# The last attention group of a cross-attention and mixture-of-experts kernel written out step by step, its row plan and output products moved, and one bf16 cast given to ScalarE

## What is computed

```python
qp = einsum('bld,ed->ble', layernorm(x), Wq)
idx = argmax(einsum('bld,bmd->blm', qp, ctx), axis=-1)      # one context row for each x row
mkv = take(ctx, idx) @ Wkv.T                                # one key and one value head, 16 wide
attn = softmax(qh @ mk.T / 4)                               # 16 heads, queries against all rows
x = x + (attn @ mv) @ Wc.T
# mixture of experts: 8 experts, 2 for each row
h = layernorm(x)
topk_w, sel = top_k(softmax(h @ router_w.T), 2)
y = (h @ w1[e, 512:].T) * silu(h @ w1[e, :512].T)           # 256 -> 512
x = x + sum over the two e of topk_w * (y @ w2[e].T)        # 512 -> 256
```

## Time and profile before

| | |
|---|---|
| median of 3 runs | 381.35 us (380.42 to 387.86) |
| the profiled execution | 383.68 us |
| its span, first to last instruction | 381.9 us |
| mean granted TensorE clock | 0.968 |
| TensorE busy | 335.8 us (88%) |
| VectorE, ScalarE, GpSimd busy | 206.0, 186.9, 191.8 us |

### The profile page before, as it was taken

One profiled execution on the slowest core, in us unless ns is written; L12 is line 12 of the kernel. 1 busy time (PEld: TensorE's weight loads), 2 busy tenths in 40 slices (PEclk: granted clock), 3 DMA queues, 4 the chain that ended last, 5 costly groups with the idle time before them and its releaser, 6 DMA issues.

```text
span 381.9 us, 7576 instructions
## 1 busy us (share of the span) xinstructions
PE 335.8 (88%) x2303; PEld 231.9 (61%) x2304; DVE 206.0 (54%) x686; ACT 186.9 (49%) x344; POOL 191.8 (50%) x212
## 2 busy tenths in 40 slices
PE   2999979989988888699899799999999999999950
PEld 2975644445544433477666577777777777777740
DVE  4668664546887757477786244434444344444420
ACT  2544347795885963354633244444444444444420
POOL 3300248777675772625873545554555554545430
PEclk9999999999989969899999899999999999999996
DMA  8999712234253365905223323333333232333321
GB/s 246 393 406 409 272 44 70 80 100 155 98 180 113 113 213 132 346 2 146 52 41 89 66 36 55 58 56 56 56 55 52 44 52 48 56 56 56 43 27 14
DMA packets 35626, 43.77 MB, mean 115 GB/s; under 512 B 3248, under 2 KB 28208, under 8 KB 35600
## 3 DMA queue, kind: packets, MB, share of 16 engines
q1 hardware_dynamic: 27024, 32.58, 24.6%
q0 software_dynamic: 7488, 10.39, 16.8%
q10 hardware_dynamic: 1088, 0.46, 0.5%
HBM read 27.49 MB, written 15.93 MB: 114 GB/s over the span
## 4 chain that ended last, share of the span: by engine, by line
PE 65%; DVE 9%; issue 8%; POOL 6%; DMA 6%; ACT 3%; ACTq 0%; POOLq 0%; DVEq 0%
PE ps L1528 25%; PE ps L1539 12%; POOL low L475 5%; PE ps L1546 5%; PE ps L1382 4%; PE ps L1252 3%; PE ps L1342 2%; DMA X<-rows,idx 2%; PE ps L1241 2%; PE ps L1514 2%; DMA pT<-in_Wq 2%; PE ps L1283 1%; PE ps L1323 1%; DVE oh L924 1%; PE ps L1350 1%
## 5 line engine op out<-in xcount | busy, mean ns | idle before, releaser
L522 POOL DMA_INDIRECT out_x<-xn,idx x39 | 62.3, 1596 | 88.6 <-ACT xn L676 84.1
L475 POOL TENSOR_TENSOR low<-raw,W 128x256 bf16<-128x256 f32 x96 | 67.2, 730 | 50.3 <-ACT W L575 47.2
L1528 PE MATMUL ps<-W,kb 128*128 x312 | 83.5, 410 | 0.1
L682 ACT ACTIVATE uT<-ps 128x512 f32<-128x512 f32 x39 | 23.3, 597 | 84.7 <-PE ps L1528 84.7
L1528 PEld LDWEIGHTS ps<-W,kb 128*128 128x128 f32 x312 | 57.1, 190 | 12.4 <-issue 0.5
L1122 DVE TENSOR_TENSOR uT<-uT,ps 128x512 f32<-128x512 f32 x39 | 26.8, 686 | 56.9 <-ACT uT L682 56.9
L1126 DVE TENSOR_TENSOR kb<-ps,mT 128x512 fp32r<-128x512 f32 x39 | 27.0, 692 | 46.8 <-ACT mT L688 46.8
L498 POOL DMA_INDIRECT X<-rows,idx x39 | 39.0, 1000 | 24.0 <-issue 11.3
L1528 PE MATMUL ps<-W1lo,kT 128*128 x156 | 40.4, 382 | 0.0
L814 DVE TENSOR_REDUCE mx<-ps 128x8 f32<-128x616 f32 x32 | 25.3, 795 | 17.9 <-PE ps L1283 17.8
L596 ACT ACTIVATE pT<-ps 77x2048 f32<-77x2048 f32 x16 | 30.0, 1873 | 7.5 <-PE ps L1323 7.5
(11 more groups left out here) (200 smaller groups left out, 537.1 us busy)
## 6 DMA issues: line engine op xcount, KB each, us to landing
raw<-in_w SPq DMA_DIRECT2D x8, 1536.0 KB, 16.4
lows<-low SPq DMA_DIRECT2D x48, 128.0 KB, 1.7
W1lo<-lows SPq DMA_DIRECT2D x8, 512.0 KB, 4.4
rows<-xr SPq DMA_DIRECT2D x4, 528.0 KB, 3.5
X<-in_x SPq DMA_DIRECT2D x4, 512.0 KB, 7.4
out_x<-X SPq DMA_DIRECT2D x4, 512.0 KB, 4.4
pT<-lows SPq DMA_DIRECT2D x8, 256.0 KB, 5.9
X<-rows,idx POOLq DMA_INDIRECT x39, 2.8
```

Of the source, the lines that this page charges most:

```text
L475: op = pool.tensor_tensor(low[:, n % LR, part], raw[:, n + 2, part], W[:, n, part].bitcast(F32), ALU.subtract)
L522: pool.indirect_dma_start(out=out[0:2 * QW, :] if c < EARLY else out, out_offset=at_rows(c), in_=ob[:, c % GR, :], in_offset=None, compute ...
L1528: mm = pe.matmul(ps[:, f, :], part[:, c * P:(c + 1) * P], chunk(wts, e * WC1 + (2 * c + f)), start=(k == 0 and c == 0), stop=(k == 2 and c ...
```

## The change

- `for u in range(NH)` becomes `range(NH - 1)` on TensorE, ScalarE and VectorE. The last group is written out.
- On TensorE both heads of group 2 and its first two combines come ahead of most of group 3, `scores_turned` of the next step stands ahead of the `turn_sums` of the last, and three fills stand between the pieces at the group's end. Heads of group 3 go to banks 1 and 3, those of group 2 to 5 and 7, and the output products of both use 5 and 7 in turn. Combines 0 and 1 of group 3 and `ranks(2)` stand ahead of `inner(0)`.
- On VectorE `places(1)` stands ahead of `normalise(2, 3)`, the eight pairs of `hots(1)` are in one piece, and the early plan follows in one piece with `normalise(3, 1)` in it. `places` is divided into `slots` and `columns`; `late_ends` gives up `late_counts`; the late plan's parts move to earlier blocks.
- One more `high` in slot 3 of groups 0 to 2; group 3 has four left, one in each of two steps and two after `sums_out(3, 2)`.
- TensorE's new `amid(b)` stands ahead of `outer(b - 1)`: ranks, place and tokens are moved into it. GpSimd's `deviations(3)` and `weights_pow(3)` stand one block earlier.
- `y_b` is cast by ScalarE from `y_hi`.

```diff
-HEADS_AT = ((5, 5), (5, 5), (5, 5), (5, 7))
-WC_AT = ((5, 5, 5, 5), (5, 5, 5, 5), (5, 5, 5, 5), (5, 7, 5, 7))
+HEADS_AT = ((5, 5), (5, 5), (5, 7), (1, 3))
+WC_AT = ((5, 5, 5, 5), (5, 5, 5, 5), (5, 7, 5, 7), (5, 7, 5, 7))
-HIGH_SLOT = (2, 2, 2, 1, 2, 1, 1, 1)
+HIGH_SLOT = (2, 2, 2, 2, 2, 1, 1, 1)
...
+            weights(1)
+            exps(3, 0)
+            heads_turned(2, 0)
+            heads_turned(2, 1)
+            exps(3, 1)
+            sums_out(3, 0)
+            x2_normal(1, (0, 1))
+            high(1)
+            exps(3, 2)
+            sums_out(3, 1)
+            x2_normal(1, (2, 3))
+            high(1)
+            exps(3, 3)
+            sums_out(3, 2)
+            high(NC)
+            sums_out(3, 3)
+            heads_turned(3, 0)
+            heads_turned(3, 1)
...
                     act.copy(y_hi, ps[:, 3, :]).then_inc(yh_ok, 1)
+                    act.wait_ge(yh_ok, b + 1)
+                    act.copy(y_b, y_hi.bitcast(F32)).then_inc(yb_ok, 1)
...
             rows_in(0)
-            heads_turned(3, 0)
-            heads_turned(3, 1)
+            x2_normal(2, range(HT))
...
+            places(1)
+            normalise(2, 3)
+            hots(1, 0, 8)
+            weighed(1)
+            residual(2, 0)
+            normalise(3, 0)
+            table(1)
+            early_blocks()
+            normalise(3, 1)
+            early_columns()
+            residual(2, 1)
+            rows_early()
+            normalise(3, 2)
+            residual(2, 2)
+            normalise(3, 3)
+            residual(2, 3)
+            choose(2)
...
             def between(b):
+                if b == 0:
+                    residual(3, 1)
                 if b == 1:
                     weighed(2)
                 if b == 2:
+                    hots(2, 3, 5)
+                if b == 3:
+                    columns(3)
+                if b == 4:
+                    hots(3, 5, 7)
+                if b == 5:
+                    weighed(3)
+                if b == 6:
+                    late_columns()
+                if b == 7:
+                    rows_late()
+            def behind(b):
+                if b == 0:
+                    residual(3, 2)
+                    hots(2, 0, 3)
+                if b == 1:
+                    residual(3, 3)
+                    choose(3)
+                if b == 2:
+                    hots(2, 5, 8)
+                    scaled(3)
+                    slots(3)
+                if b == 3:
+                    hots(3, 0, 5)
+                if b == 4:
+                    hots(3, 7, 8)
+                    table(2)
                     plan_used()
+                    late_counts()
                 if b == 5:
                     late_ends()
+                    table(3)
+                    late_blocks()
...
+            scores_turned(3, 0)
+            turn_sums(2, 3)
+            fill(7, 2)
+            turn_heads(2, 0)
+            turn_heads(2, 1)
+            fill(4, 2)
+            scores_turned(3, 1)
+            sums(3, 0)
+            combine(2, 0)
+            combine(2, 1)
+            scores_turned(3, 2)
+            turn_sums(3, 0)
+            place(1)
+            sums(3, 1)
+            scores_turned(3, 3)
+            combine(2, 2)
+            turn_sums(3, 1)
+            sums(3, 2)
+            fill(6, 2)
+            tokens(0)
+            turn_sums(3, 2)
+            combine(2, 3)
+            pe.wait_ge(ex_ok, NH * STEPS)
+            fill(0, 3)
+            sums(3, 3)
+            fill(0, 3)
+            turn_sums(3, 3)
+            fill(0, 3)
+            turn_heads(3, 0)
+            turn_heads(3, 1)
+            fill(0, 3)
+            combine(3, 0)
...
             def aside(b):
                 if b == 0:
-                    combine(3, 1)
+                    combine(3, 2)
                 if b == 1:
-                    combine(3, 2)
                     combine(3, 3)
+            def amid(b):
+                if b == 2:
+                    ranks(3)
+                    totals(1)
                 if b == 3:
                     place(2)
-                    ranks(3)
-                    totals(1)
-                if b == 6:
+                if b == 5:
                     place(3)
                 if b == 7:
                     tokens(1)
...
             turn_rows(0, 16)
-            fill(1, 2)
-            turn_sums(3, 3)
-            fill(1, 3)
-            turn_heads(3, 0)
-            turn_heads(3, 1)
+            ranks(2)
+            combine(3, 1)
             inner(0, expert(0))
-            combine(3, 0)
```

More of the change, by code:

```diff
@@ L645, in x2_normal @@
                                    scale=rs2[:, i:i + 1]).then_inc(xn2_ok, 1)
-            for u in range(NH):
+            for u in range(NH - 1):
                 for k in range(SLOTS):
@@ L891, in _, with ranked, slots @@
             LINKS = 6
-            def places(v):
-                done = [LINKS * v]
-                def link(ins):
-                    done[0] += 1
-                    ins.then_inc(rt_l, 1)
-                    dve.wait_ge(rt_l, done[0])
+            def ranked(v, n, ins):
+                ins.then_inc(rt_l, 1)
+                dve.wait_ge(rt_l, LINKS * v + n)
+            def slots(v):
                 dve.wait_ge(pre_mm, v + 1)
@@ L1126, in y_lows @@
                 dve.tensor_tensor(y_lo, ps[:, 3, :], y_hi.bitcast(F32), ALU.subtract).then_inc(yl_ok, 1)
-                dve.tensor_copy(y_b, y_hi.bitcast(F32)).then_inc(yb_ok, 1)
             def step(i, blocks, last):
@@ L1470, in tokens @@
                 at, n = (EARLY, LATE) if g else (0, EARLY)
-                pe.matmul(ps[:, 7, 456:456 + n], tab[:], pickb[:, at:at + n], start=True, stop=True).then_inc(idx_mm, 1)
-            for u in range(NH):
+                pe.matmul(ps[:, 7 if g else 6, 456:456 + n], tab[:], pickb[:, at:at + n], start=True, stop=True).then_inc(idx_mm, 1)
+            for u in range(NH - 1):
                 for k in range(SLOTS):
                     v = u - 1
-                    if u + 1 < NH and k == 7:
+                    if k == 7:
                         turn_maxima(u + 1)
@@ L1501, in _ @@
                         combine(v, 3)
-                    if u == 3 and k == 2:
-                        place(1)
-                    if u == 3 and k == 5:
-                        tokens(0)
                     if u >= 1 and k == 7:
```

111 lines of the change are left out of this document (40 added, 71 removed).

## The result

| | before | change |
|---|---|---|
| median (20 runs each) | 383.47 us (378.11 to 388.60) | 378.63 us (374.67 to 383.69) |
| the profiled execution | 383.68 us | 380.34 us |
| its span | 381.9 us | 378.5 us |

The ratio is 0.9878, 95% interval 0.9847 to 0.9909: 1.2% faster, where I had forecast 2.4% (372.4 us, range 367 to 378.5). The time lies 0.13 us above the range. Part of the distance is the base: I took 9.0 us off the 381.35 us of the three runs shown, while twenty runs of the kernel before have a median of 383.47, from which the same 9.0 would give 374.5. So of the 6.2 us between 372.4 and 378.63, 2.1 are the base; the rest is the gain, 4.8 us between the medians where 9.0 was forecast.

A forecast was written before the change was run, and what follows sets the result against it. TensorE held 65% of the chain; the gain stood in the last attention group and first ten blocks. 2.6 + 6.8, less 0.4 for hand-overs, gave 9.0 us off 381.35: 372.4 us, range 367 to 378.5.

The forecast's parts named there:

- Blocks: Blocks 0 to 9, inner(0) to inner(10): 54.2 us against 60.99, a gain of 6.8 us, bounds 2.2 and 7.5.
- a late gather 9: Blocks 4 to 6: a VectorE chore slips, row numbers stay late, 4.6 us of gain is gone: 377 us, chance 0.15.
- each is 4.9 plus what lies in it: Blocks 0 to 9: each takes 4.9 us plus its combine, place or ranks, and 0.1 to 0.2 of VectorE's lateness.
- One more high in slot 3: Groups 0 to 2: ScalarE may be held 0.5 to 2.3 us, covered by TensorE's other work; cost 0.
- VectorE's order: Group 3: places(1), slowed beside GpSimd's lows, delays turn_heads(2, 0); 1.75 us of loss, bounds 0 and 2.0.
- The clock falls there: Group 3, pause before turn_heads(2, 0): TensorE drops to half clock behind it, costing 1.5 us, bounds 0 and 3.5.
- rival (a): Group 3: the clock holds through fills, or places(1) slips between lows; 1.5 to 3.2 us more gain, chance 0.25.
- The walk of group 3: Group 3, piece by piece at full clock: inner(0) at 154.5, with both losses 157.8 instead of 160.4; gain 2.6 us.
- y_b: Every block: ScalarE's cast takes about 0.58 us against 0.48 on VectorE, covered by 1.4 us; effect 0.
- Steady block unchanged at 4.9: Expert blocks after the first ten: each still takes 4.9 us; any movement would make the forecast wrong.
- VectorE's stalls: Blocks 0 to 9: the rest of the 6.8 us gain, after 4.6 for gather 9 and 2.1 for two combines.
- rival (d): Group 3: many short waits keep TensorE at half clock throughout; about 385 us, all 27 us giving 395; chance 0.04.

The follow-up runs named there:

- e14_x2: The change with x2_normal(2) put back behind y_hi(0) and y_hi(1) instead of ahead of Silu(0): 375.54 us, ratio 0.9793 to the kernel before.
- e4_numbers: The change with rows_late ahead of gated(7) on VectorE instead of behind rows_low(8): 376.08 us, ratio 0.9820 to the kernel before.
- e16_tok: The change with edits to highs, normalise, row numbers, gathers and x2_normal, and the late plan one step earlier: 369.81 us, ratio 0.9673 to the kernel before.

## Why the prediction was wrong

The step that failed by most is the one for the blocks, a gain of 6.8 us of which 2.1 came; the one for the highs, put at 0, failed too.

- *Blocks: gain 6.8, bounds 2.2 and 7.5.* Measured 2.07, at the lower bound, which was meant for a late gather 9 that did not come about. The step "each is 4.9 plus what lies in it" left out GpSimd's queue: the power of 5.47 us that moved one block earlier put gather 6 behind it (2.7 us with the clock). And "tokens(1) goes ahead of outer(6), and the row numbers come about when inner(8) begins" was right to 0.4 us (205.80 and 205.43), the gather's wait of 0.4 measured 0.55; missing were the register loads of 1.23 us. Those two blocks are 4.5 of the 4.6 us by which the sum is off. With both mended (and the highs, the order, the gathers and x2_normal) the blocks took 54.00, against the 54.2 forecast.
- *One more high in slot 3: 0, bounds 0 and 1.8.* Wrong, and the bounds too. I wrote that TensorE reaches the sums only after work that takes as long. In group 0 it does not: it waited 1.00 us for exps, and there the clock fell. The stretch lost 0.8 us where the clock held and 4.1 to 4.8 where not. I had weighed the wait for a low, not the high behind that wait, nor the clock.
- *VectorE's order: 1.75 of loss.* Right: the pause was 1.81 with links at 0.65, and the swap gave 1.4 back.
- *The clock falls there: 1.5.* Wrong, rival (a) came true, and its first reason has support: the run without fills fell to 0.80 and its group 3 lost 4.4 us. But that the clock held was also luck, since in one of six executions with the same pause and fills it fell. I took the length of a pause for the cause from the one execution that I read. In that same trace, outside the rows shown, the clock fell behind a pause of 1.55 us at 107.36 and held behind one of 1.53 at 118.05, and in two other executions of the old order it held behind the 1.83.
- *The walk of group 3.* It was 1.2 us too long besides, spread over all pieces: heads, sums(3, 1), sums(3, 2) and sums(3, 3) came 0.3, 0.6, 0.7 and 1.0 us sooner after scores(3, 0) than I had them. The waits at sums(3, 2) (0.8) were as forecast.
- *y_b: 0.* Right by two runs.
- *Steady block unchanged at 4.9.* Right; the end took 160.90 for 160.67.
- *The base.* Three runs gave 381.35 and twenty 383.47: 2.1 us of the distance, and no fault of the walk. Without it the time would have been inside the range, with a gain of about half of what I forecast.

Two slips of arithmetic changed little. The 4.6 us that I gave to the gather in blocks 8 and 9 are 4.2 by the starts used there (9.25 and 5.45 us against 5.5 and 5.0), and 4.0 by starts from the timeline, where inner(9) is at 215.60 and not 215.94; VectorE's stalls are then 0.5 or more of the 6.8, not 0.1. And 27 us at half clock in rival (d) would have given about 398, not 395.

Added up: 9.0, plus 2.7 for group 3, less 4.7 for the blocks, less 0.8 for the highs, plus 0.2 at the end, is a gain of 6.4 us where group 0's clock holds, and 3.1 where it falls. The profiled execution of the change is one of the second kind (3.4 between the spans, with the 0.3 of an earlier start), and the 4.8 between the medians of twenty runs lie between the two. That the time came so near the range is thus in part two errors of opposite sign, group 3's 2.7 and the blocks' 4.7. Not settled: why the same pause is followed by half clock in some executions and not in others, and how much of e14_x2's median is its edit.

## What to carry to other kernels

Price a chore that is put ahead of an instruction for which TensorE waits by what is queued behind it, its own wait included, and count the half-clock stretch that even a pause of 1.0 us can set off. Fills on both sides of a pause are cheap where a clock is at stake (here eighteen products for some 3 us), but they are no guarantee, and one profiled execution does not show whether a clock falls at a place. For a DMA that waits on late data, having it land in time isn't enough: in this kernel rows that landed 0.4 us before TensorE turned them left the register loads behind the wait open, and rows that landed 3.3 us before did not; and a transfer that needs nothing of a slow neighbour in its queue belongs ahead of it.

## What the runs showed of the hardware

- Half clock behind a pause does not follow from the pause's length alone. In slot 3 of group 0 it came behind 1.00, 1.03 and 1.09 us and not behind 0.81 or less. A pause of 1.53 to 1.55 us in group 2, the same in all seventeen profiles, was followed by half clock, within 1.7 us, in fourteen of them (not in the change, e4_numbers and e16_tok). The clock held behind 2.45 us in the change, and behind 1.81 or 1.82 with fills around it in five executions of six.
- In five runs turn_y(0) waited 2.1 us; in two of them the products behind it ran at full clock, in three at half for a while.
- Three 128x8 links on VectorE of 0.65 us each beside GpSimd's lows, 0.17 alone (the earlier trace rows for the same line).
- Register loads on TensorE show only when its stream is held up: 0.68 and 0.55 us once in block 8, nothing in e16_tok.
